# Graph network kernel on one Trainium2 core: bucket count with 128 weight columns, and last blocks zeroed in 19 indirect calls

## The reference, cut to what matters

```python
def reference(x, src, dst, edge_attr_128, edge_type_3, edge_weight, ...):
    edge_index = jnp.stack([src, dst])
    x = _layernorm(x + _L0_gnn_ref(...))   # segment mean of edge_attr over src, three linear + batch norm
    x = _layernorm(x + _L1_gnn_ref(...))   # segment mean of x[src] over dst, one linear
    x = _layernorm(x + _L2_gnn_ref(...))   # typed messages W[type] of (x[src], x[dst]), mean over dst
    x = _layernorm(x + _L3_gnn_ref(...))   # weighted, degree-normalised sum over dst
    return x
```

## Time and profile before

| What | Value |
|---|---|
| Median of 3 runs | 4548.34 us |
| Span of the profiled execution | 4017.3 us |
| Outside the span, median less span | 531.0 us |
| PE busy | 2953.8 us |
| DVE busy | 2455.1 us |
| POOL busy | 1923.7 us |
| ACT busy | 1140.9 us |
| Mean DMA rate | 183 GB/s |

### The profile page before, as it was taken

One profiled execution on the slowest core, in us unless ns is written; L12 is line 12 of the kernel. 1 busy time (PEld: TensorE's weight loads), 2 busy tenths in 40 slices (PEclk: granted clock), 3 DMA queues, 4 the chain that ended last, 5 costly groups with the idle time before them and its releaser, 6 DMA issues.

```text
span 4017.3 us, 86931 instructions
## 1 busy us (share of the span) xinstructions
PE 2953.8 (74%) x22101; PEld 2579.0 (64%) x22102; DVE 2455.1 (61%) x6376; ACT 1140.9 (28%) x3541; POOL 1923.7 (48%) x1875
## 2 busy tenths in 40 slices
PE   7455444444368886776888799999969976787996
PEld 7233222222258855776887499999958866776995
DVE  6666666666657775333777654444447874334887
ACT  0111000000023344554222332222123037788003
POOL 3777777777720034776000067777754006774000
PEclk9999999999999988998999899999989978998998
DMA  6444444444468815786775244444457826776883
GB/s 190 144 145 143 142 143 146 146 142 143 136 198 250 250 43 184 268 274 217 241 240 175 103 157 160 161 160 161 136 164 221 262 73 223 264 274 206 269 268 117
DMA packets 431358, 736.75 MB, mean 183 GB/s; under 512 B 71749, under 2 KB 207566, under 8 KB 430270
## 3 DMA queue, kind: packets, MB, share of 16 engines
q1 hardware_dynamic: 336846, 498.35, 40.7%
q0 software_dynamic: 94448, 237.72, 16.2%
HBM read 486.89 MB, written 294.76 MB: 195 GB/s over the span
## 4 chain that ended last, share of the span: by engine, by line
PE 34%; POOL 28%; issue 18%; DMA 11%; DVE 4%; ACT 2%; DVEq 1%; POOLq 1%; SPq 0%; ACTq 0%
PE ps L1257 23%; POOL slots L685 18%; DMA gbuf<-ring_raw,to_blk 8%; POOL gbuf L733 6%; POOL ring_raw L738 3%; PE ps L1289 2%; PE ps L1300 2%; PE ps L1136 2%; DMA ring_raw<-msg_rows,tables 2%; PE ps L1337 1%; PE ps L1328 1%; PE ps L1409 1%; ACT ring_raw L890 1%; DVE stats L1745 1%; PE ps L1393 1%
## 5 line engine op out<-in xcount | busy, mean ns | idle before, releaser
L733 POOL DMA_INDIRECT gbuf<-ring_raw,to_blk x731 | 752.0, 1029 | 784.0 <-ACT ring_raw L893 427.6
L1257 PE MATMUL ps<-ring_raw,hot_raw 128*128 128x128 f32 (+2 forms) x6576 | 819.7, 281 | 137.0 <-DVE hot_raw L1681 49.8
L1257 PEld LDWEIGHTS ps<-ring_raw,hot_raw 128*128 128x128 f32 x6576 | 774.4, 193 | 190.7 <-issue 131.2
L685 POOL DMA_INDIRECT slots<-ring_raw,idx_edges x782 | 763.3, 976 | 241.3 <-issue 241.3
L1681 DVE TENSOR_TENSOR hot_raw<-dst_lane,lane_ids 128x1024 f32<-128x1024 f32 x516 | 636.7, 1235 | 89.6 <-ACT dst_lane L866 49.2
L1289 PE MATMUL ps<-big,hot_raw 128*128 x5160 | 584.6, 276 | 21.5 <-ACT ring_raw L893 17.7
L1289 PEld LDWEIGHTS ps<-big,hot_raw 128*128 128x128 f32 x5160 | 578.9, 192 | 27.6 <-issue 27.5
L1171 PE MATMUL ps<-big 128*49 128x343 bf16 (+6 forms) x784 | 263.4, 489 | 405.2 <-DVE big L1577 403.9
L1691 DVE TENSOR_TENSOR big<-big,ps 128x128 f32 (+2 forms) x1032 | 297.1, 288 | 277.3 <-PE ps L1257 193.9
L1171 PEld LDWEIGHTS ps<-big 128*49 128x49 bf16 x784 | 113.9, 159 | 547.9 <-DVE big L1577 313.8
L893 ACT COPY ring_raw<-ps 128x512 f32<-128x512 f32 x473 | 277.4, 587 | 646.3 <-DMA gbuf<-ring_raw,to_blk 409.8
(11 more groups left out here) (262 smaller groups left out, 3713.3 us busy)
## 6 DMA issues: line engine op xcount, KB each, us to landing
ring_raw<-gbuf SPq DMA_DIRECT2D x669, 268.0 KB, 3.2
ring_raw<-in_edge_attr SPq DMA_DIRECT2D x111, 448.0 KB, 3.9
zr<-lane_rows SPq DMA_DIRECT2D x129, 384.0 KB
ring_raw<-slots SPq DMA_DIRECT2D x153, 272.0 KB, 3.1
zt<-lane_rows SPq DMA_DIRECT2D x86, 384.0 KB
big<-slots SPq DMA_DIRECT2D x105, 272.0 KB, 2.9
big<-gbuf SPq DMA_DIRECT2D x105, 268.0 KB, 3.1
pays_raw<-key_rows SPq DMA_DIRECT2D x112, 224.0 KB
```

The lines of the kernel that those rows point to most:

```text
L685: pool.indirect_dma_start(edges, bass.IndirectOffsetOnAxis(idx_edges[0:n, u, j:j + 1], 0), edge_rows[0:n, u, j, :], None).then_inc(scatter ...
L733: pool.indirect_dma_start(gbuf, bass.IndirectOffsetOnAxis(to_blk[:, t:t + 1], 0), node_rows[:, r, :], None, bounds_check=NBLK - 1, oob_is_ ...
L1257: ins = pe.matmul(bank(r % 3, width), hots[:, r, j * P:(j + 1) * P], rows[:, j, 0:width], start=j == 0, stop=j == BLK - 1)
```

## The change

The weights of the count matmuls become 128 columns. The view that they come from now runs on over both halves of `hot1` (source one-hots, then destination one-hots), so that a stride of seven from `j` meets 128 elements: the 98 of before and 30 of the destination half. The patch in PSUM becomes 128 x 98. Its last 30 rows are not read; the copy reads the same 98 x 98.

The 2401 entries of `last_b` are no longer padded to 2450. They are read back as 127 lanes x 19: one DMA for 126 full lanes, and one for the 7 entries of the last lane. The 12 places of that lane that no DMA writes are set to `NOWHERE` by a POOL memset of the whole tile, early on. That memset raises `consts`, so SP waits for 13 of them instead of 12. The indirect calls are 19 of 127 lanes. POOL waits for three DMAs on `last_out` instead of two. The DVE instruction that wrote the fiftieth column is gone.

```diff
-LASTB = 25
-LASTP = 98
-assert LASTB * LASTP == GROUPS * (GROUPS + 1)
+LASTB = 19
+LASTP = -(-GROUPS * GROUPS // LASTB)
+LASTN = GROUPS * GROUPS - (LASTP - 1) * LASTB
+assert LASTP <= P
...
-            sp.wait_ge(consts, 12)
+            sp.wait_ge(consts, 13)
...
             sp.dma_start(last_blocks, last_b[:, :]).then_inc(last_out, 16)
             sp.wait_ge(last_out, 16)
-            sp.dma_start(zero_idx[:, :], last_blocks.rearrange("a b -> (a b)").rearrange(
-                "(p k) -> p k", k=LASTB)).then_inc(last_out, 16)
+            flat = last_blocks.rearrange("a b -> (a b)")
+            sp.dma_start(zero_idx[0:LASTP - 1, :], flat[0:(LASTP - 1) * LASTB].rearrange("(p k) -> p k", k=LASTB)).then_inc(
+                last_out, 16)
+            sp.dma_start(zero_idx[LASTP - 1:LASTP, 0:LASTN], flat[(LASTP - 1) * LASTB:].rearrange(
+                "(p k) -> p k", k=LASTN)).then_inc(last_out, 16)
...
             pool.tensor_copy(ident_h[:, :], ident[:, :]).then_inc(consts, 1)
+            pool.memset(zero_idx[:, :], int(NOWHERE)).then_inc(consts, 1)
...
-            pool.wait_ge(last_out, 32)
+            pool.wait_ge(last_out, 48)
...
-                left, right = (hot1[:, s, k].rearrange("p g c -> p (g c)") for k in range(2))
+                both, right = hot1[:, s].rearrange("p k g c -> p (k g c)"), hot1[:, s, 1].rearrange("p g c -> p (g c)")
                 for j in range(HB // 2):
-                    ins = pe.matmul(ps[0:PAIR, 0, 0:PAIR], left[:, j::HB // 2], right[:, j::HB // 2],
+                    ins = pe.matmul(ps[:, 0, 0:PAIR], both[:, j:j + P * HB // 2:HB // 2], right[:, j::HB // 2],
                                     start=first_of(b) and j == 0, stop=True, skip_group_check=True)
...
-            mark(dve.tensor_scalar(last_b[:, GROUPS:GROUPS + 1], heads[:, 0:1], 0.0, NOWHERE, ALU.mult, ALU.add))
```

More of the change, by code:

```diff
@@ L177, in gnn_kernel @@
         src_rows = dram("src_rows", [COLS, P], BF16)
-        last_blocks = dram("last_blocks", [GROUPS, GROUPS + 1], U32)
+        last_blocks = dram("last_blocks", [GROUPS, GROUPS], U32)
         X = sb("X", [P, GROUPS, D])
@@ L286, in gnn_kernel @@
         heads_i = sb("heads_i", [GROUPS, 2], I32)
-        last_b = sb("last_b", [GROUPS, GROUPS + 1], U32)
+        last_b = sb("last_b", [GROUPS, GROUPS], U32)
         zero_idx = sb("zero_idx", [LASTP, LASTB], U32)
```

## The result

The changed kernel takes 4622.55 us (median of 4 runs, 4616.43 to 4635.64), the kernel before 4548.77 us (4 runs beside them, 4545.37 to 4559.36). The ratio is 1.0158, 95% interval 1.0135 to 1.018: 73.8 us or 1.6% slower. Forecast were 4539.2 us, range 4529 to 4552.

The account below looks back on a forecast made before the run. One thread up to the first edge scatter, then POOL's scatters at their own pace, bound the kernel. Terms -8.0 + 0.2 + 0.3 - 0.1 - 1.5 = -9.1 us took 4548.3 to 4539.2 us, range 4529 to 4552.

Parts of the forecast that it names:

- So lanes are free: Zeroing calls: more lanes don't lengthen a POOL call, so six fewer calls save 7.6 to 9.3 us, taken as 8.0.
- A call now has 8 blocks for the busiest of 16 engines, not 7: Zeroing: the last landing of 2.76 us grows by 0 to +0.4 us, taken as +0.2.
- the signs: Zeroing: the forecast is wrong if call spacing exceeds 1.3 us or the last landing exceeds 4 us.
- The rival of transfers: Zeroing bound by its transfers: fewer calls wait longer at the landing, the gain vanishes, about 4547 us; chance 0.09.
- The second read: Reading back the last blocks before zeroing: one more DMA costs 0 to +0.4 us, taken as +0.3.
- The memset: POOL's early fill of the 127 x 19 index tile: 0.1 to 0.35 us, covered by POOL's idle time, so 0.
- The long call: Zeroing call at 123.62 us, the 22nd: its 1.68 us extra might fall away, making the saving 9.3 instead of 7.6 us.
- The count: Count matmuls: moving columns set the spacing; the 128-wide load shortens 23 rounds by 0.065 us each, -1.5 us.
- the gain of -14.8 us: Count matmuls: the weight load sets the spacing, 28 rounds give -14.8 us, in all 4525.9 us; chance 0.07.
- the loss of +14.6: Count matmuls: striding slows the wide load, spacing 0.23 us, +14.6 us there, total 4555.3 us; chance 0.08.
- The carry to the end: Edge scatters: POOL waits for nobody, so every microsecond saved ahead of them reaches the end at full value.
- 531.0 us that the median leaves over the span: Whole kernel: time outside the profiled span of 4017.3 us, added to it to give 4548.3 us before the change.

Follow-up runs that it names:

- n128_again: Changed kernel with 128 lanes a zeroing call (lane 127 outside the table), repeated on a third chip: 4589.92 us, ratio 0.9969 to the kernel before.
- b_again: The kernel before, nothing edited, profiled once more: 4552.72 us.
- n128: Changed kernel with its 19 zeroing calls 128 lanes wide instead of 127, lane 127 outside the table: 4545.74 us, ratio 0.9973 to the kernel before.

## Why the prediction was wrong

**The step that failed** is "So lanes are free", on which the -8.0 us of six fewer calls stood. It drew a line through 98 lanes (0.962 us) and 128 lanes (0.958 us), and took 127 to lie on it. The same step stands once more in the next paragraph of the prediction, "A call now has 8 blocks for the busiest of 16 engines, not 7", which gave +0.2 us for the last landing: it spread 127 rows over 16 engines as if they were 128. But the cost follows the largest divisor up to 16, which is 14 for 98, 16 for 128 and 1 for 127. Both rows it rested on were cheap for a reason that the new number lacks, and no row of before had a count with a small divisor. An unknown shape was priced by its two neighbours, with no bound kept for it: this term had a range of 1.7 us, and was off by more than 80. In place of -8.0 + 0.2 us stand +76.8 us from the first call to the first scatter (112.4 for 35.6). Six calls fewer did save 7.3 us, as the same 19 calls of 128 lanes show (28.3 us). Against those, 127 lanes cost 84.1 us: 19 x 1.57 = 30 us of longer calls, 41 us of two pauses, and 16.8 us for 3.1 us of waiting behind the last call. The prediction had named the signs itself, a spacing over 1.3 us (it is 2.85) and a last landing over 4 us.

The Trainium skill says it outright, in DMA: Bandwidth & Descriptors, section Why a DMA increments its semaphore by 16 and not by 1: the number of engines is the largest k up to 16 that divides the outer dimension, and its list of examples gives 1 for 127 partitions. The trace agrees, with 15 x 63 packets of 8 bytes a call; the prediction made no use of it. The same section of the Trainium skill also tells of an exception for some direct copies issued by POOL, which spread 127 partitions over 16 engines. These indirect ones don't: 17955 packets of 8 bytes. And by the same section of the Trainium skill, POOL's transfers with k below 16 take their engines in turn. The overlap of a batch fits that: up to seven pairs were under way at once, in a batch of seven calls. But seven side by side still took 85 ns a pair, half of the 168 ns of one record and not a seventh; what held them up isn't shown.

**The rival of transfers** ("the zeroing is bound by its transfers", 0.09) named the right place with the wrong price: it let the gain vanish, at 4547 us, and had no way to be slower than before. Against it stood "rows 6 and a DMA share of 0.55". The first has 128 lanes, the second is a mean over engines. Neither could speak of 127.

**The second read** of the last blocks was priced about right. From the issue of the first read to POOL's first call the profile after has 2.98 us (90.64 to 93.61), the profile before 2.59 (92.96 to 95.55): +0.39 for +0.3. But the nine profiles with two reads have 2.66 to 2.98 us and the three with one read 2.57 to 2.76, so one pair of profiles can't fix it. **The memset** took 0.529 us in the profile after, over its bound of 0.35, and 0.530 in n128_again; in the seven other profiles that have it, it took 0.11. It lies in the idle time that was named for it: 0. **The long call** of 2.64 us, for which 0.4 us were added to the saving, belonged to one execution: b_again has none over 1.79 us.

**The count** was right in its mechanism. The moving columns set the spacing: loads halved (254 to 133 ns), matmuls stayed, and matmuls of a group still start 0.158 us apart (60.679, 60.837, 60.995 us in the trace). Both rivals on it fall, the gain of -14.8 us and the loss of +14.6. The prediction's estimate had 82 and 27 ns for the two loads, with nothing for the stride; here they take 254 and 133, and the measurement decides. The size was a little short: last matmul from 85.04 to 82.77 us, -2.3 us for -1.5, since a round shortened by 0.11 us (the lower bound's number) and not by 0.065. It lies in the lead of the first load: after a wait for DVE the second matmul started 0.267 us behind the first, and now 0.158 to 0.166; the median spacing is 0.158 us before and after.

**The carry to the end** held for the loss: +74.8 us at the first scatter, +68.0 at the last (1410.1 to 1478.1), +63.5 in the span, +73.8 in the medians. For the gain, n128 has -10.0 us at the first scatter, -7.1 at the last, -1.4 in one span and -12.3 (0.27%) by the ratio of the times; the times carry it, single spans differ by more than that. "POOL waits for nobody", the reason that the prediction gave, is true on the kind of chip that it read and false where the times were taken. On the first kind the scatters take 1000.6 to 1000.9 us from first to last in all five profiles, whether they start at 125.7 or at 201.6, so there a shift is carried in full. On the other kind they take 1271.6 to 1300.4 us in seven profiles, and the carry can't be read to better than some 10 us.

**The frame.** "531.0 us that the median leaves over the span" isn't time outside the span: that is 2 us. It was, by all signs, the distance between two chips. It would have shifted no difference here, but a gap of 13% between a profile's span and the median was a question to ask, not a term to add.

## What to carry to other kernels

Before changing the number of lanes of an indirect transfer, factor it: counts with a divisor of 11, 14 or 16 cost here what their calls cost, while primes (101, 127) and 2 x 61 made each call longer, slowed the transfers and made POOL pause. A lane that points outside the table is the cheap cure: from 127 to 128 lanes won 73 us, measured side by side (4663.09 and 4589.92 us). Where a term extrapolates to a size that no row has, keep the outcome "another regime" in the range, even if the rows on both sides agree.

## What the runs showed of the hardware

- The chip moves an 8-byte packet for every engine that the rule leaves idle and every pair of rows: 945 in a call of 127 lanes, at 1.69 ns of POOL's time each. A call of 98 to 128 lanes takes POOL about 0.87 us and 0.83 ns for each of 16 x lanes / k rows (from the seven lane counts).
- Calls of 127 lanes overlap, with up to seven pairs of rows under way, and yet a batch of seven takes 37 us.
- POOL can stand still between calls for 22 us with no semaphore to show for it, and goes on for a whole batch of calls afterwards (7, then 7, then 5), not call by call.
- Weights of 128 strided bf16 columns load in 133 ns, 98 of them in 254; the matmuls stay 0.158 us apart.
- One program takes about 4011, 4559 or 4601 us on three different chips. Of the difference between the first two, 278 us lie in the edge scatters (1001 us against 1279), where DVE, at 643 and 664 busy us, is waited for on the one chip alone. The granted clock in that stretch is 1.00 on both. The cause stays open.
